# One-core graph and attention kernel: matrix additions begun per pair, second norm derived from the first, stream statistics taken per tile

## The reference

```python
xn = _layernorm(x)                                  # first norm, eps 1e-5
# graph branch, two layers, on xn
w = einsum('rb,bio->rio', att, basis)               # 2 relations from 30 bases
for r in range(2):
    gate = sigmoid(x_j @ gate_w[r]); msgs.append(gate[:, None] * x_j @ w[r])
agg = segment_sum(where(edge_type == 0, msgs[0], msgs[1]), row); h = agg + x @ root + bias
# attention branch, two layers (i = 0, 1), on xn
y = layernorm(x, ln1_g[i], ln1_b[i])                # norm of the stream
q, k, v = y @ Wq + bq, y @ Wk + bk, y @ Wv + bv
qp, kp = softmax_kernel(q), softmax_kernel(k)       # 256 random features a head
x = x + (ctx of kp and v, read by qp, normalised) @ Wo[i] + bo[i]
y = layernorm(x, ln2_g[i], ln2_b[i])                # statistics of the new stream
x = x + gelu(y @ W1[i] + b1[i]) @ W2[i] + b2[i]
# then x + both branches, a norm, and a product-key memory with top-8 search and row gathers
```

## Time and profile before

| what | value |
|---|---|
| median of 3 runs | 2818.54 us (2815.58 to 2827.08) |
| profiled execution, its own time | 2807.37 us |
| its span, first to last instruction | 2805.3 us |
| PE busy | 2551.7 us, 91% of the span |
| DVE, ACT, POOL busy | 53%, 25%, 37% |
| mean granted clock of PE | 0.974 |
| chain that ended last | PE 78%, DVE 10%, DMA 5%, unknown queue 2% |

### The profile page before, as it was taken

How to read it: one execution, slowest core, us unless ns; L and a number is a source line. 1 busy time by engine, 2 the same in 40 slices (tenths; PEclk the granted TensorE clock), 3 DMA queues, 4 the chain that set the end, 5 groups by cost and what they waited for, 6 DMA issues and landing times.

```text
span 2805.3 us, 25699 instructions
## 1 busy us (share of the span) xinstructions
PE 2551.7 (91%) x8620; PEld 1400.3 (50%) x8620; DVE 1479.4 (53%) x3776; ACT 707.5 (25%) x1651; POOL 1042.4 (37%) x887
## 2 busy tenths in 40 slices
PE   2999979999499999999999978999989989998877
PEld 2666656765244444445656656545445445443321
DVE  4665675455376500001335634577677677677664
ACT  0346231211010011001454311333323323322322
POOL 0005877774021100000000000566656656656665
PEclk9999989999799999999999989999999999999999
DMA  8924144548776520431005000889988988989998
GB/s 283 302 67 124 3 91 111 116 91 171 189 205 186 152 58 0 130 101 55 1 1 169 1 8 8 281 309 318 334 304 317 332 311 307 336 322 337 360 354 331
DMA packets 235961, 524.29 MB, mean 187 GB/s; under 512 B 99362, under 2 KB 99737, under 8 KB 231675
## 3 DMA queue, kind: packets, MB, share of 16 engines
q0 software_dynamic: 170032, 379.99, 41.7%
q1 hardware_dynamic: 63257, 137.66, 16.2%
q10 hardware_dynamic: 2550, 5.12, 0.5%
HBM read 489.51 MB, written 45.34 MB: 191 GB/s over the span
## 4 chain that ended last, share of the span: by engine, by line
PE 78%; DVE 10%; DMA 5%; issue 3%; another core or an unknown queue 2%; ACT 1%; POOL 1%; SPq 0%; POOLq 0%; DVEq 0%; ACTq 0%
PE bank L1304 13%; PE bank L1056 12%; PE bank L892 5%; PE bank L903 5%; PE bank L1284 5%; PE bank L1294 4%; PE bank L1033 4%; PE bank L668 3%; PE bank L560 3%; PE bank L774 3%; PE bank L1241 3%; PE bank L567 2%; PE bank L574 2%; PE bank L1043 2%; PE bank L600 2%
## 5 line engine op out<-in xcount | busy, mean ns | idle before, releaser
L1385 ACT ACTIVATE stage<-ident,qv 125x125 f32<-125x125 f32 x640 | 246.3, 398 | 513.9 <-DVE qv L1538 184.5
L1304 PE MATMUL bank<-qv,stage 125*125 125x512 f32 x640 | 338.9, 619 | 32.9 <-ACT stage L1385 16.1
L1538 DVE SCALAR_TENSOR_TENSOR qv<-qv 125x512 f32<-125x512 f32 x320 | 238.0, 750 | 150.6 <-DMA qv<-in_L_ffn_rows,biasb 71.2
L285 POOL DMA_INDIRECT adj<-e_cnt,e_idx x80 | 164.3, 2054 | 275.7 <-issue 238.0
L1204 POOL MEMSET wreg<- 64x2048 f32 x2 | 3.6, 1801 | 688.3 <-DVE h L699 688.2
L1210 POOL DMA_INDIRECT qv<-in_L_ffn_rows,qv x160 | 162.5, 1016 | 217.6 <-issue 140.2
L1304 PEld LDWEIGHTS bank<-qv,stage 125*125 125x125 f32 x640 | 111.1, 190 | 180.9 <-issue 113.6
L1210 POOL DMA_INDIRECT qv<-in_L_ffn_rows,biasb x160 | 161.3, 1008 | 99.8 <-PE bank L1304 71.4
L285 POOL DMA_INDIRECT adj_b<-e_cnt,e_idx x80 | 174.7, 2184 | 38.9 <-issue 26.2
L1304 PE MATMUL bank<-big,stage 125*125 125x512 f32 x320 | 166.8, 617 | 12.7 <-issue 6.5
L1056 PE MATMUL bank<-big,wreg 125*125 125x512 f32 x400 | 172.0, 592 | 0.0
(11 more groups left out here) (224 smaller groups left out, 4211.1 us busy)
## 6 DMA issues: line engine op xcount, KB each, us to landing
wreg<-in_L_gnn_basis SPq DMA_DIRECT2D x30, 1024.0 KB
stage<-in_L_gnn_basis POOLq DMA_DIRECT2D x45, 512.0 KB, 4.4
big<-in_L_mix_W SPq DMA_DIRECT2D x4, 4096.0 KB
adj<-adj_b POOLq DMA_DIRECT2D x9, 1328.1 KB, 41.2
adj<-wreg SPq DMA_DIRECT2D x5, 2187.5 KB
adj_b<-wreg SPq DMA_DIRECT2D x5, 2187.5 KB
wreg<-adj SPq DMA_DIRECT2D x10, 1093.8 KB
qv<-adj SPq DMA_DIRECT2D x10, 1093.8 KB
```

The costliest lines, as they stand in the source:

```text
L285: nc.gpsimd.indirect_dma_start(out=(adj, adj_b)[g % 2], out_offset=bass.IndirectOffsetOnAxis(ap=e_idx[:, g:g + 1], axis=0), in_=e_cnt[:, g ...
L1304: nc.tensor.matmul(psum[7][0:P, :], diags[:, s % DRING, :], ring[s % RING][0:P, DIM:ROW], start=(s == 0), stop=(s == SLOTS - 1), skip_grou ...
L1385: nc.scalar.activation(diags[:, s % DRING, :], ident[0:P, 0:P], ACT.Relu, scale=inner[:, s:s + 1]).then_inc(p_diag, 1)
L1538: nc.vector.scalar_tensor_tensor(ring[s % RING][0:P, 0:DIM], ring[s % RING][0:P, 0:DIM], probs_of[t % 2].rearrange("p h k -> p (h k)")[:, ...
```

## The change

The change has five parts.

1. `edge_index_dve` is called in each pair for that pair's 32 groups, and POOL waits at every 32nd addition for that pair's indices only. The zeroed copies are still awaited first.
2. For layer 0, the second norm's variance is computed from the first: the variance of the normed input is the first variance times the square of its reciprocal deviation, and its mean is set to 0. The ten `bn_stats` and ten `bn_aggr` of `ln1_dve` are gone there; `rsqrt` stays.
3. The `bn_stats` of the input stand ahead of the edge work in `setup_dve`.
4. The statistics of the stream for the second norm of each layer are taken in `attn3_dve`, one tile two steps after its output is added, in both layers.
5. The nine loads of small vectors and the two of `att` go from SP's queue to ACT's for layer 0 (`setup_act`); in layer 1 they stay on SP, behind the projection's.

```diff
--- before.py
+++ after.py
@@ -276,10 +276,11 @@
         CONSTS = 9 + 2
 
         def adjacency_pool(pool):
-            pool.wait_ge(s_idx, 4)
             pool.wait_ge(s_adjz, 5 * 64)
 
             for g in range(GROUPS):
+                if g % CHUNK == 0:
+                    pool.wait_ge(s_idx, 4 * (g // CHUNK) + 4)
                 if g >= 2:
                     pool.wait_ge(s_adj[g % 2], g // 2 * 16)
                 nc.gpsimd.indirect_dma_start(
@@ -296,8 +297,6 @@
                 sp.dma_start(h[rows, :, :], tok(a["x"])[rows, :, :]).then_inc(s_xin, 16)
             for n, name in enumerate(("src", "dst", "edge_type_2")):
                 sp.dma_start(e_raw[:, n, :], a[name].rearrange("(p g) -> p g", p=P)).then_inc(s_edge, 16)
-            sp.dma_start(att_b[:, 0, :], a["L0_gnn_att1"].rearrange("r b -> (r b)").partition_broadcast(128)).then_inc(s_att, 16)
-            sp.dma_start(att_b[:, 1, :], a["L0_gnn_att2"].rearrange("r b -> (r b)").partition_broadcast(128)).then_inc(s_att, 16)
             attn_loads_sp(sp, 0)
             sp.wait_ge(s_cellsb, 2)
             sp.dma_start(cells_t[0:128, :], cell_ts[:, 0, :]).then_inc(s_cellw, 16)
@@ -316,6 +315,9 @@
             wo_load_sp(sp, 0)
 
         def setup_dve(dve):
+            dve.wait_ge(s_xin, 32)
+            for t in range(TILES):
+                nc.vector.bn_stats(st6[:, t, :], h[:, t, :]).then_inc(s_ln, 1)
             dve.wait_ge(s_edge, 48)
             nc.vector.tensor_copy(e_f, e_raw).then_inc(s_cell, 1)
             dve.wait_ge(s_cell, 1)
@@ -339,9 +341,6 @@
             nc.vector.tensor_copy(cell_ts[:, 0, :], psum[0][:, 0:P]).then_inc(s_cellsb, 1)
             nc.vector.tensor_copy(cell_ts[0:GROUPS - 128, 1, :], psum[0][0:GROUPS - 128, 128:128 + P]).then_inc(s_cellsb, 1)
 
-            dve.wait_ge(s_xin, 32)
-            for t in range(TILES):
-                nc.vector.bn_stats(st6[:, t, :], h[:, t, :]).then_inc(s_ln, 1)
             dve.wait_ge(s_ln, TILES)
             for t in range(TILES):
                 nc.vector.bn_aggr(mv[:, t, :], st6[:, t, :]).then_inc(s_ln, 1)
@@ -359,18 +358,20 @@
                 nc.vector.scalar_tensor_tensor(part, part, cell[:, ds(i * CHUNK + n, 1)], wmask,
                                                ALU.is_equal, ALU.mult, accum_out=code[:, ds(i * CHUNK + n, 1)]).then_inc(s_code, 1)
 
-        def edge_index_dve(dve):
-            dve.wait_ge(s_code, GROUPS)
-
-            nc.vector.tensor_copy(e_cnt[:, :], code).then_inc(s_idx, 1)
-            nc.vector.tensor_scalar(flag, code, 256.0, None, ALU.is_ge).then_inc(s_cell, 1)
-            nc.vector.tensor_copy(trash, trash.bitcast(I32)).then_inc(s_cell, 1)
-            dve.wait_ge(s_cell, 12)
-            nc.vector.tensor_tensor(trash, trash, cell, ALU.subtract).then_inc(s_idx, 1)
-            dve.wait_ge(s_idx, 2)
-            nc.vector.tensor_tensor(trash, trash, flag, ALU.mult).then_inc(s_idx, 1)
-            dve.wait_ge(s_idx, 3)
-            nc.vector.tensor_tensor(e_idx[:, :], trash, cell, ALU.add).then_inc(s_idx, 1)
+        def edge_index_dve(dve, i):
+
+            some = slice(CHUNK * i, CHUNK * i + CHUNK)
+            dve.wait_ge(s_code, CHUNK * (i + 1))
+
+            nc.vector.tensor_copy(e_cnt[:, some], code[:, some]).then_inc(s_idx, 1)
+            nc.vector.tensor_scalar(flag[:, some], code[:, some], 256.0, None, ALU.is_ge).then_inc(s_cell, 1)
+            nc.vector.tensor_copy(trash[:, some], trash[:, some].bitcast(I32)).then_inc(s_cell, 1)
+            dve.wait_ge(s_cell, 12 + 2 * i)
+            nc.vector.tensor_tensor(trash[:, some], trash[:, some], cell[:, some], ALU.subtract).then_inc(s_idx, 1)
+            dve.wait_ge(s_idx, 4 * i + 2)
+            nc.vector.tensor_tensor(trash[:, some], trash[:, some], flag[:, some], ALU.mult).then_inc(s_idx, 1)
+            dve.wait_ge(s_idx, 4 * i + 3)
+            nc.vector.tensor_tensor(e_idx[:, some], trash[:, some], cell[:, some], ALU.add).then_inc(s_idx, 1)
 
         def setup_pe(pe):
             pe.wait_ge(s_const, CONSTS)
@@ -381,7 +382,7 @@
 
 
 
-        ADDS = dict(w=13 * 16, pj=32, pjT=1, pjS=4, v1=1, stat=2 * TILES + RSQ, z=TILES, yT_pe=KC * PAIRS, yT=KC * PAIRS, q_pe=KC * PAIRS,
+        ADDS = dict(w=13 * 16, pj=32, pjT=1, pjS=4, v1=1, stat=3 + RSQ, z=TILES, yT_pe=KC * PAIRS, yT=KC * PAIRS, q_pe=KC * PAIRS,
                     sq=2 * KC * PAIRS, k=KC * PAIRS, k_pe=KC * PAIRS, v_pe=TILES, v=TILES, dg_mm=PAIRS, dgc=PAIRS, dg_pe=PAIRS, dg=2 * PAIRS,
                     kd_pe=4 * TILES, kmx=4 * TILES, kd=4 * TILES, gmx=5, gmx_pe=2, kx=2 * TILES, kf=2 * TILES, ctx_pe=4, cT=2, cTa=2, cT_pe=4, ctx=4,
                     qd_pe=4 * TILES, qm=4 * TILES, qn=4 * TILES, qx=4 * TILES, qT_pe=4 * TILES, qT=4 * TILES, o_pe=2 * TILES,
@@ -411,13 +412,19 @@
             for n, name in enumerate(("Wq", "Wk", "Wv")):
                 sp.dma_start(wreg[:, n, :].rearrange("p (k n) -> p k n", k=KC),
                              a["L0_mix_" + name][l].rearrange("(k p) n -> p k n", p=128)).then_inc(m["w"], 16)
-            for c, name in ((c_g1, "ln1_g"), (c_b1, "ln1_b"), (c_g2, "ln2_g"), (c_b2, "ln2_b"), (c_bq, "bq"), (c_bk, "bk"), (c_h1, "b1")):
-                sp.dma_start(c, a["L0_mix_" + name][l].rearrange("(k p) -> p k", p=128), allow_slow_non_contiguous=True).then_inc(m["w"], 16)
-            for b, name in ((b_v, "bv"), (b_o, "bo")):
-                sp.dma_start(b, a["L0_mix_" + name][l].partition_broadcast(P)).then_inc(m["w"], 16)
-
             for s in range(2):
                 sp.dma_start(proj_st[:, :, 64 * s:64 * s + 64], a["L0_mix_proj"][l].rearrange("(k p) d -> p k d", p=128)).then_inc(m["pj"], 16)
+
+        def attn_vectors(queue, l):
+            for c, name in ((c_g1, "ln1_g"), (c_b1, "ln1_b"), (c_bq, "bq"), (c_bk, "bk"), (c_g2, "ln2_g"), (c_b2, "ln2_b"), (c_h1, "b1")):
+                queue.dma_start(c, a["L0_mix_" + name][l].rearrange("(k p) -> p k", p=128), allow_slow_non_contiguous=True).then_inc(m["w"], 16)
+            for b, name in ((b_v, "bv"), (b_o, "bo")):
+                queue.dma_start(b, a["L0_mix_" + name][l].partition_broadcast(P)).then_inc(m["w"], 16)
+
+        def setup_act(act):
+            attn_vectors(act, 0)
+            act.dma_start(att_b[:, 0, :], a["L0_gnn_att1"].rearrange("r b -> (r b)").partition_broadcast(128)).then_inc(s_att, 16)
+            act.dma_start(att_b[:, 1, :], a["L0_gnn_att2"].rearrange("r b -> (r b)").partition_broadcast(128)).then_inc(s_att, 16)
 
         def mlp_loads_sp(sp, l):
             sp.wait_ge(m["ctx"], l * ADDS["ctx"] + 4)
@@ -465,7 +472,13 @@
                 dve.wait_ge(s_ln, LN0_DONE)
             nc.vector.memset(v_aug[:, :, :, HD:HD + 1].rearrange("p t h o -> p (t h) o"), 1.0).then_inc(m["v1"], 1)
             if l == 0:
-                ln1_dve(dve, 0)
+                nc.vector.tensor_tensor(rs[:, 2, :], rs[:, 0, :], rs[:, 0, :], ALU.mult).then_inc(m["stat"], 1)
+                nc.vector.memset(mv[:, :, 0:1].rearrange("p t o -> p (t o)"), 0.0).then_inc(m["stat"], 1)
+                dve.wait_ge(m["stat"], 2)
+                nc.vector.tensor_tensor(mv[:, :, 1], mv[:, :, 1], rs[:, 2, :], ALU.mult).then_inc(m["stat"], 1)
+                dve.wait_ge(m["stat"], 3)
+                rsqrt(dve, m["stat"], 3, mv[:, :, 1], 0, TILES)
+                dve.wait_ge(m["stat"], 3 + RSQ)
             dve.wait_ge(m["w"], l * ADDS["w"] + W_LOADS)
 
             def norm1(t):
@@ -506,6 +519,8 @@
                         spread(i)
                         if not last:
                             norm1(2 * i + 2)
+                    if l == 0 and n == (3 if i else 7):
+                        edge_index_dve(dve, i)
 
             dve.wait_ge(m["kmx"], l * ADDS["kmx"] + 4 * TILES)
             nc.vector.tensor_reduce(kmax_all, kmax.rearrange("p t h -> p h t"), AX, ALU.max).then_inc(m["gmx"], 1)
@@ -519,9 +534,6 @@
             dve.wait_ge(m["dg"], l * ADDS["dg"] + 2 * PAIRS)
             nc.vector.scalar_tensor_tensor(kshift, diag[:, :, 1, :], -1.0, kmax_all.unsqueeze(1).to_broadcast([P, TILES, HEADS]),
                                            ALU.mult, ALU.subtract).then_inc(m["gmx"], 1)
-            if l == 0:
-                edge_index_dve(dve)
-
         def attn1_pe(pe, l):
             pe.wait_ge(m["pj"], l * ADDS["pj"] + 32)
             if l == 0:
@@ -698,7 +710,7 @@
                 dve.wait_ge(m["hat"], l * ADDS["hat"] + 2 * T + 3)
                 nc.vector.tensor_tensor(h[:, T, :], h[:, T, :], b_o, ALU.add).then_inc(m["hat"], 1)
 
-            for n in range(UNITS + 7):
+            for n in range(UNITS + 10):
                 if n < UNITS:
                     T, c = n // KC, n % KC
                     dve.wait_ge(m["qd_pe"], l * ADDS["qd_pe"] + n + 1)
@@ -719,6 +731,14 @@
                     normalize((n - 4) // 4, (n - 4) % 4 // 2)
                 if n >= 10 and n % 4 == 2:
                     residual((n - 10) // 4)
+                if n >= 12 and n % 4 == 0:
+                    T = (n - 12) // 4
```

(15 more changed lines are left out.)

## The result

The kernel after takes 2780.26 us (2772.08 to 2783.30) against 2819.16 before: ratio of the runs 0.9874, 95% interval [0.9851, 0.9897], some 35 us. Run once more beside the experiments it gave 0.9866 [0.9849, 0.9882]. The forecast, 2773 us, was a saving of 45.8; the range held the time.

A forecast was written before the change was run, and what follows sets the result against it. PE, busy for 91% of the span, was taken as the bound, so only its idle stretches could be saved. Savings of 9.7 + 11.9 + 24.2 = 45.8 us off the 2818.5 us median gave 2773 us, range 2752 to 2796.

The forecast's parts named there:

- Part 1: The start (statistics first, second norm from the first, loads on ACT's queue): 9.7 us saved, 6.7 to 11.9.
- the two norms: Second norms of both layers, nine of ten statistics moved behind earlier outputs: 6.1 and 5.8 us saved, 11.9 together.
- part 3: Additions start earlier, so the sum of the copies is issued at 614 instead of 661: 24.2 of 39.8 us saved.
- the plain sum: Whole kernel: savings of the start, second norms and additions added, 9.7 + 11.9 + 24.2 = 45.8 us.
- 4.7 + 8 us: Graph layer's start: last base combined 4.7 us after landing, then some 8 us of loads by SP.
- `root` and the tiles, some 8 us: Ahead of the graph layer, SP's loads of root (1 MB) and small ones take some 8 us.
- the 45 packets of rows 9: Queue 1 beside the sum, 45 packets in 4 us: read as tiles of 125 rows with little in flight.
- Rival A: Base loads keep pace with the sum, graph layer starts on time: 61.4 us saved, 2757 us; chance 0.27.
- The 45 against 169 of rows 9: Packets of queues 1 and 0 in 4 us beside the sum: taken to speak for single turns, not bursts.
- Rival B: Additions slower early on, 3.0 us each, sum some 11 us later: 34.6 us saved, 2784 us; chance 0.17.
- Rival D: Sum starves, each load packet holding it up 0.6 us on its engine: +23 us, 2842 us; chance 0.04.
- The zeroing: Zeroing of the copies, begun 5 us earlier, ends at about 156 us instead of 160.86; first addition then.

The follow-up runs named there:

- first profile: The kernel after, unchanged, in the first of its two profiled executions; span 2781.5 us.
- run 11: Kernel after, but POOL's clearing of the block-diagonal keys is cut in two halves, the first running much earlier; 0.9856 of the kernel before.
- run 2: Kernel after, but in both layers the stream's statistics are taken for all ten tiles after the last output, as before; 0.9875 of the kernel before.
- run 3: Kernel after, but layer 0's second norm takes its ten statistics and ten aggregations again; 0.9861 of the kernel before.
- run 5: The kernel after once more, unchanged, as control of the experiments; 0.9866 of the kernel before.
- run 4: Kernel after, but the eleven small loads stand in SP's queue again, as before the change; 0.9881 of the kernel before.
- run 1: Kernel after, but POOL waits for the indices of all five pairs ahead of its first addition, as before; 0.9906 of the kernel before.
- run 8: The kernel of run 1 with the gate weights loaded before the MLP instead of behind root; 0.99 of the kernel before.
- run 9: The kernel of run 6 with each tile of xn_d loaded as 112 and 13 rows instead of 125; 0.9809 of the kernel before.
- run 12: The kernel of run 9 with later half combinations, the bias loaded in 112 and 13 rows, and POOL's clearing cut in two; 0.9766 of the kernel before.
- run 6: Kernel after, but POOL issues the sum behind four half bases, root, gates and two tiles; DVE's half combinations spread later; 0.986 of the kernel before.

## Why the prediction was right in total and wrong in a step

- **Part 1** gave 9.0 us for 9.7 and the two norms 6.5 and 3.5 for 6.1 and 5.8, each read at its own place. The missing 2.3 us are DVE's two steps beside POOL's clearing (first profile), of which run 11 gave back 1.5. The statistics moved beside the outputs cost nothing that shows.
- **The steps that failed are the price of part 3 and, with it, the plain sum**, "9.7 + 11.9 + 24.2". The forecast had the graph layer's start follow the last base by 4.7 + 8 us. That came true where the sum was over when the last base landed (runs 2, 3, 5), and fell where it still ran (first profile, runs 4, 11). What holds in all six is the distance to the sum's issue, 82 to 86 us. Undoing the norm of layer 0 and the statistics moved the MLP's end by 6 and 8 us and that distance by under 4, and cost nothing and 2.5 us (runs 3, 2). By these traces a saving on layer 0 that doesn't bring the sum forward is in part lost. How much is not shown: the intervals allow a cost of 6 and of 10 us, and each of these kernels has one trace.
- **The size of part 3.** The forecast's other parts bring the aggregation from 839.98 to 824.2 (9.7 + 6.1 earlier), and it began at 821.16 (run 1). With part 3 it should have been at 800.0, and it was at 812.99, 802.64 and 804.37 (first profile, runs 5, 11). That is 8.2, 18.5 and 16.8 us for 24.2; by the times it is 9 to 11, at most 18. Without part 3 the change gives 26 us (21 to 32), where the forecast's other parts make 21.6. So in the total, 35 to 38 us for 45.8, the errors partly cancel, which is luck.
- **"`root` and the tiles, some 8 us"** was right where the sum had ended by then (8.6 us from the last combination's end at 673.0 to 681.64) and wrong beside it (18.9 us, from 673.3 to 692.20). Beside the sum, the gate weights take 1024 turns and a tile of 125 rows gets a third of the packets. I had passed over the gate weights as "small ones", and taken the 45 packets of rows 9 for a sign that little was in flight. Runs 8, 9 and 12 show that it was the form of the transfer.
- **Rival A** (the loads keep pace) fell with the 14.6 us a load. By the Trainium skill (DMA: Bandwidth & Descriptors, section on queues, rings and completion order) they would come in bursts of 9 to 17 descriptors; the 16 and 16 packets in 0.47 us speak for single turns. The 45 against 169 of rows 9, which the prediction took as its evidence, came of the five engines. **Rival B** (3.0 us an addition) fell too: beside the comparisons the first 16 took 2.4 us each (166.20 to 203.91, first profile). **Rival D** (the sum starves) had the right mechanism, a turn for every packet, but too high a price: in 15 us of turns q0 still moved 2.46 MB, 0.66 in 4 us where it has 0.84 alone. Its 0.6 us a packet stands on no row.
- **The zeroing** was to end at 156 because it began earlier. It began 4.2 us earlier (55.3 instead of 59.5) and ended at 157.7 to 167.5, before the change at 160.86. The sum's issue followed the first addition by 434 to 444 us in seven traces, so both the zeroing and the additions' own time move it. Of the 12.5 us between the sums of the two profiles, 7.5 came from the first addition.

## What to carry to other kernels

Where a large transfer runs beside the loads that an engine waits for, count packets and not bytes: a load's time is its number of packets times a turn, divided by the engines that its rows lie on, so a 4-byte element costs nearly as much as 2 KB (187 against 147 in 4 us). Before adding up savings, find the one event behind which the next stage starts; what lies on another branch can be swallowed by the wait. And when a long transfer is moved earlier, ask what it now runs beside: issued behind the few loads that are needed at once it gained nothing by itself (run 6), and 1.0% once the forms of the transfers and the clearing were mended too (run 12). The early sum with mended transfers was not run, so what the later issue is worth by itself stays open.
